# Sandwich transformer kernel, rotation tables made on GpSimd for two blocks at once, and the second residual placed inside the root step on VectorE

## What is computed

```python
x = attn_layer(shift_tokens(x), Wqkv[i], q_scale[i], k_scale[i], Wo[i]) + x   # first residual
x = ffn_layer(shift_tokens(x), ...) + x                                      # second residual

q = l2norm(q) * qs ;  k = l2norm(k) * ksc
q = q * cos * scale + rotate_half(q) * sin * scale
k = k * cos * inv   + rotate_half(k) * sin * inv
out = local_attention(q, k, v)      # windows of 32 tokens, 16 heads of 64
```

## Time and profile before

| | us |
|---|---|
| median of 3 runs | 1886.04 (1882.17 to 1889.05) |
| the profiled execution: its time | 1887.05 |
| the profiled execution: its span | 1885.2 |

### The profile page before, as it was taken

How to read it: one execution, slowest core, us unless ns; L and a number is a source line. 1 busy time by engine, 2 the same in 40 slices (tenths; PEclk the granted TensorE clock), 3 DMA queues, 4 the chain that set the end, 5 groups by cost and what they waited for, 6 DMA issues and landing times. The chain is left out here.

```text
span 1885.2 us, 76475 instructions
## 1 busy us (share of the span) xinstructions
PE 1674.5 (89%) x30960; PEld 1193.9 (63%) x30960; DVE 1578.2 (84%) x2345; ACT 1221.7 (65%) x2072; POOL 1483.0 (79%) x819
## 2 busy tenths in 40 slices
PE   3946878899999999999999999999999999999974
PEld 2523556666766676667667666676676766776663
DVE  5787767789889898898998888989989889898854
ACT  3334556567677776777777767777767677776753
POOL 1638767778888888888888888888888888888841
PEclk8878989999999999999999999999999999999997
DMA  3001131122223222323221332222242223222210
GB/s 133 1 1 45 49 99 48 47 67 60 63 74 104 58 56 64 78 69 89 64 67 45 87 102 67 67 53 70 67 111 57 54 67 78 66 58 65 67 47 23
DMA packets 80698, 121.88 MB, mean 65 GB/s; under 512 B 16776, under 2 KB 29574, under 8 KB 79750
## 3 DMA queue, kind: packets, MB, share of 16 engines
q1 hardware_dynamic: 80646, 121.14, 24.4%
HBM read 19.36 MB, written 1.05 MB: 11 GB/s over the span
## 5 line engine op out<-in xcount | busy, mean ns | idle before, releaser
L729 PE MATMUL r<-wqkv,xs 128*128 (+1 forms) x1152 | 561.2, 618 | 13.0 <-DVE rot_sin L1246 3.7
L1433 POOL TENSOR_TENSOR rot<-rot,root 128x1024 f32<-128x1024 f32 x192 | 377.9, 1988 | 120.6 <-DVE root L1284 120.6
L1405 POOL TENSOR_TENSOR rot<-rot,rot_sin 128x1024 f32<-128x1024 f32 x192 | 451.8, 2365 | 1.2 <-DVE rot_sin L1246 1.2
L729 PEld LDWEIGHTS r<-wqkv,xs 128*128 128x128 f32 x1152 | 210.5, 196 | 213.0 <-issue 197.6
L1079 ACT ACTIVATE squares<-r 128x512 f32<-128x512 f32 x384 | 217.6, 598 | 83.9 <-PE r L729 82.8
L1235 DVE TENSOR_TENSOR rot<-r,table 128x1024 f32<-128x1024 f32 x192 | 232.7, 1212 | 23.0 <-PE r L734 10.2
L1418 POOL TENSOR_TENSOR squares<-squares 128x512 f32<-128x512 f32 x192 | 244.8, 1275 | 9.0 <-ACT squares L1079 8.8
L1449 POOL TENSOR_TENSOR probs<-probs,rinv 128x1024 f32<-128x1024 f32 x96 | 182.8, 1905 | 81.0 <-DVE rinv L1306 81.0
L1246 DVE TENSOR_TENSOR rot_sin<-r,table 128x512 f32<-128x512 f32 x384 | 242.6, 672 | 0.0
L734 PE MATMUL r<-square,rot 128*128 128x128 f32 x1536 | 208.1, 279 | 19.5 <-POOL rot L1433 14.0
L734 PEld LDWEIGHTS r<-square,rot 128*128 128x128 f32 x1536 | 169.5, 141 | 83.8 <-issue 29.9
(11 more groups left out here) (125 smaller groups left out, 2688.5 us busy)
## 6 DMA issues: line engine op xcount, KB each, us to landing
vwin<-vtok SPq DMA_DIRECT2D x576, 128.0 KB, 2.3
vwin<-vtok SPq DMA_DIRECT2D x384, 64.0 KB, 2.0
wqkv<-in_wqkv SPq DMA_DIRECT2D x6, 1536.0 KB, 8.3
wo<-in_wo SPq DMA_DIRECT2D x6, 512.0 KB, 4.9
w<-in_w SPq DMA_DIRECT2D x6, 341.0 KB, 3.0
x<-in_x SPq DMA_DIRECT2D x4, 256.0 KB, 3.7
rope<-in_rope SPq DMA_DIRECT2D x1, 1024.0 KB
out_x<-y SPq DMA_DIRECT2D x4, 256.0 KB, 2.3
```

What stands on the lines that cost most here:

```text
L729: pe.matmul(dst[:, c * 512:(c + 1) * 512], xs1[:, u, :], w.rearrange("p a n -> p (a n)"), start=True, stop=True).then_inc(S[done], 1)
L1405: pool.tensor_tensor(r, r, rot_sin[:, k, :, :, :].rearrange("p h a d -> p h (a d)"), ALU.add)\
L1433: pool.tensor_tensor(r, r, bcast(root[:, at:at + HEADS], 2, DH), ALU.mult)\
```

## The change

Two things are changed. The table product leaves DVE: POOL makes it, for both blocks of a pair in one instruction of 128x512, one pair ahead, between `fold_q` 1 and `weigh` 0; the table has a second buffer that pairs take in turn, so the DVE readers pick theirs by an address computed at run time. And `find_roots` is split: `residual2` now stands behind the first root step and ahead of the seed.

```diff
-        table = sb("table", [P, 2, 4, DH])
+        table = sb("table", [P, 2, 2, 4, DH])
...
             def turn_cos(n, u, k, src, squared, turned, transposed):
-                dve.wait_ge(S["tabled"], n + 1)
+                dve.wait_ge(S["tabled"], n // 2 + 1)
...
-                                  bcast(table[:, u, 2 * k, :], 1, HEADS), ALU.mult).then_inc(S[turned], 1)
+                                  bcast(table[:, bass.ds((n // 2) % 2, 1), u, 2 * k, :].rearrange("p a d -> p (a d)"),
+                                        1, HEADS), ALU.mult).then_inc(S[turned], 1)
...
-                    sin = table[:, u, 2 * k + 1, 32 * a:32 * a + 32]
+                    sin = table[:, bass.ds((n // 2) % 2, 1), u, 2 * k + 1, 32 * a:32 * a + 32]\
+                        .rearrange("p a d -> p (a d)")
...
-                    tables(2 * m, 0)
-                    tables(2 * m + 1, 1)
...
-                    find_roots(m)
+                    begin_roots(m)
                 if runs(m - 4):
                     residual2(m - 4)
+                if runs(m) or runs(m - 2):
+                    finish_roots(m)
...
+            def tables(m):
+
+                if not isinstance(m, int) or m >= 2:
+                    pool.wait_ge(S["q_turned"], 6 * (m - 1))
+                    pool.wait_ge(S["k_turned"], 6 * (m - 1))
+                pool.tensor_tensor(table[:, bass.ds(m % 2, 1), :, :, :].rearrange("p a u k d -> p (a u) (k d)"),
+                                   rope[:, bass.ds((m % PPB) * 2, 2), :, :].rearrange("p a k d -> p a (k d)"),
+                                   bcast(scales[:, bass.ds(m // PPL, 1), :, :].rearrange("p a k d -> p (a k d)"), 1, 2),
+                                   ALU.mult).then_inc(S["tabled"], 1)
...
                     fold_q(2 * m + 1, 1)
+                if runs(m + 1):
+                    tables(m + 1)
...
-            run(pool, step)
+            pool.wait_ge(S["tables_loaded"], 7 * 16)
+            tables(0)
+            run(pool, step, PAIRS - 1)
```

More of the change, by code:

```diff
@@ L653, in first, with run @@
             return isinstance(n, int) and n == 0
-        def run(eng, step):
+        def run(eng, step, end=PAIRS):
             for m in range(FILLED):
                 step(m)
-            with eng.Fori(FILLED, PAIRS) as m:
+            with eng.Fori(FILLED, end) as m:
                 step(m)
-            for m in range(PAIRS, PAIRS + BEHIND):
+            for m in range(end, PAIRS + BEHIND):
                 step(m)
@@ L1253, in norm_square, with begin_roots @@
                                   [:, :, 0, :], AX.X, ALU.add).then_inc(S[summed], 1)
-            def find_roots(m):
+            def begin_roots(m):
                 before = ROOT_OPS * m
@@ L1267, in find_roots, with finish_roots @@
                        .then_inc(S["refined"], 1 if runs(m) else 2)
+            def finish_roots(m):
+                before = ROOT_OPS * m
                 dve.wait_ge(S["refined"], before + 2)
```

## The result

| | us |
|---|---|
| changed kernel, median of 4 runs | 1913.35 (1909.4 to 1916.38) |
| kernel before beside it, median of 4 runs | 1887.55 (1882.17 to 1892.4) |
| ratio | 1.0136, 95% interval 1.0101 to 1.0171 |
| profiled execution of the changed kernel: time, span | 1914.91, 1913.1 |

What follows compares the result with a forecast made beforehand. The bound was taken to be a loop through several engines, none full. 42 x 0.56 = 23.5 less 41 x 0.26 = 10.7 gives +12.8 us, with +0.3 for start and end: median 1899, 8-in-10 range 1879 to 1910.

Steps and rivals of the forecast that it cites:

- Gain on `turn_q` 1: On PE, `turn_q` 1 no longer waits for DVE's tables to free r0: 0.26 us gained a step.
- POOL's product: Table product on POOL ahead of `weigh` 0: 1.27 us, covered by idle before `weigh` 1, cost on the loop 0.
- the estimate weighed beside it: From the skill's GpSimd page: POOL's product takes 1.6 us, PE loses 0.3 a step, total 13 us higher.
- The register work of the table's readers: Twelve table readers with run-time addresses, 0.10 to 0.26 us each, hidden where the engine is busy: taken as 0.
- both gains: 0.26 us on `turn_q` 1 and some 0.3 on POOL's scales: POOL free for the product at about 933.9.
- `residual2` in the roots: On DVE the seed waits behind residual2, which waits for `ff_down`: 0.56 us a step, wholly on the loop.
- The step that failed: PE's idle 1.25 us before `ff_up` 0 is not on the loop, since `turn_q` 0 waits for the scale anyway.
- The drain: In steps behind the loop residual2 no longer follows nine Newton instructions: worth under 1 us, +0.3 together with the start.
- The first cos product: On DVE, expected directly behind the roots, with DVE's idle time up by about 3.5 us a step.
- A, the residual hides: Residual2 fits before the seed's wait for POOL ends: cost 0, gain 0.26 stays, -11 us, 1875; 15 in 100.
- B, a wash: Residual2 costs 0.18 against 0.26, 1883; or `turn_q` 1 gains 0.5 against 0.56, 1889; 22 in 100.
- C, POOL's product as the brake: Product at 2.34 us delays `weigh` 1 and PE, `ff_down` some 0.8 later: 34 us on top, 1933; 7 in 100.

Runs made afterwards that it cites:

- the pair with `ff_up` 0 issued twice: Matmuls of `ff_up` 0 issued twice in the changed kernel, 1898.92 us, and in the kernel before with only residual2 moved, 1910.22 us.
- the one with less work: Kernel with only the tables moved, half of `ff_up` 0 left out and one q 0 projection matmul cut from 512 to 128 columns: 1891.59 us.
- the fast kernel: Changed kernel with residual2 put back behind the roots, so only the tables are on POOL: 1872.88 us.
- the run with fixed addresses: Changed kernel with residual2 at fixed addresses, writing over its own PSUM input, so x is not updated: 1884.35 us.
- the run behind `weigh` 0: Kernel with only the tables moved, POOL's table product placed behind `weigh` 0 instead of ahead of it: 1873.47 us.
- the run behind `weigh` 1: Kernel with only the tables moved, POOL's table product placed behind `weigh` 1 instead of ahead of `weigh` 0: 1935.0 us.

## Why the prediction was right in its steps and wrong in its sum

**The loop and its terms.** These held. Gain on `turn_q` 1: 0.26 forecast, 1.13 to 0.87 measured, 0.32 a step in all with the tables alone. POOL's product: 1.27 forecast, 1.28 measured and not the 1.6 of the estimate weighed beside it, with 0.51 idle left before `weigh` 1 (0.5 forecast). The register work of the table's readers, put at 0, shows no cost: with it the step still gained the 0.32. Two figures beside the sum were off: with both gains counted POOL would have been free for the product at 933.6 and not 933.9, and DVE's busy time fell by 30.49 - 25.15 = 5.3 us a step and not by some 3.5, since the seed no longer waits for POOL. The timeline of POOL in the changed kernel:

```profile
975.96 1.28 POOL L1416 TENSOR_TENSOR squares<-squares 128x512 f32<-128x512 f32 x1
977.19 1.28 POOL L1450 TENSOR_TENSOR table<-rope,scales  x1
978.42 1.91 POOL L1457 TENSOR_TENSOR probs<-probs,rinv 128x1024 f32<-128x1024 f32 x1
980.85 1.91 POOL L1457 TENSOR_TENSOR probs<-probs,rinv 128x1024 f32<-128x1024 f32 x1 [0.51 <-DVE rinv L1304]
```

`residual2` in the roots: 0.56 forecast, 3.09 - 2.50 = 0.59 measured, and the distance from `ff_down` 0.43 forecast, 988.69 - (986.66 + 1.56) = 0.47 measured. In the timelines of PE and DVE:

```profile
986.66 1.56 PE L827 MATMUL pm<-hid,w 128*128 128x256 f32 x6 [0.18 <-DVE minus_half L1261]
...
988.69 0.48 DVE L1332 SCALAR_TENSOR_TENSOR xT<-pm,cols,mid 128x256 f32 x1 [2.25 <-PE pm L827]
989.09 0.19 DVE L1272 TENSOR_SCALAR root<-minus_half 128x67 int32<-128x67 int32 x1
...
995.00 1.23 DVE L1228 TENSOR_TENSOR rot<-r,table 128x1024 f32<-128x1024 f32 x1 [3.35 <-PE r L734]
```

The step came out at 34.41 for 34.44.

**The step that failed** is the sentence on PE's idle time: "That idle is not on the loop: `turn_q` 0 behind it waits for the scale anyway." As a wait it is not. The idle before `turn_q` 0 was even foreseen, but priced at nothing, and the sum held every PE duration at what it was in a kernel whose loop has the clock at 1.00. With 2.45 us not busy in a step instead of 1.73, TensorE's clock fell eight times in the loop, which is 14.1 us that stand nowhere in the sum, and was lower in the drain. The runs that tell this from a wait are the pair with `ff_up` 0 issued twice: the same steps, no long ones, and loops 14.0 and 17.7 us shorter; and the one with less work, which has the step of the fast kernel and the drops of the slow one. Why idle time lowers the clock in just these steps is not shown.

**The drain** was put at under 1 us, and with the start at +0.3; it cost 4.85. Ahead of the `turn_q` 0 behind the last scale of the loop PE had idled 3.47 us, and it ran at the lower clock:

```profile
1826.70 1.94 PE L734 MATMUL r<-square,rot 128*128 128x128 f32 x8 [3.47 <-POOL rot L1431]
```

```profile
1824.66:1913.10 88.44, 54.83 (x828) 43.10 (x828) 35.23 (x75) 36.95 (x59) 20.10 (x12) 0.79 0.11 30
```

The eight transposes take 1.94 us there, 1.10 in the loop. The same stretch of the kernel before has a clock of 0.87, and PE busy 50.56 of its 83.59 us. With `ff_up` 0 issued twice the stretch takes 85.80 us at a clock of 0.85, so at least 2.6 of the 4.85 go with the idle time and the clock; that the clock makes up the rest is argued, not shown by a run. The fill, 1.9 us shorter, hid a part of this; by the scatter of the fill between executions that is luck.

**The first cos product** was to start directly behind the roots with the tables gone. It does not: it waits 3.35 us for `turn_q` 0, which must have read `rot` before the product may overwrite it. In the kernel before, `turn_q` 0 ended at 915.88 + 1.09 = 916.97 and the tables at 914.81 + 3.34 = 918.15, so only some 1.2 us of their 3.58 were not covered by this wait, and taking them away frees little, whatever their 150 us of busy time. The forecast's sum did not use that sentence, since it had taken 0.26 from `turn_q` 1 alone.

**The rivals.** A, the residual hides, needed an earlier first root step: the run with fixed addresses shows the residual at a cost of 0.16 even at the shortest distance, close to the 0.18 given as the lower bound. B, a wash, would have been that case, 1884 (forecast 1883). C, POOL's product as the brake, fell with the product's 1.28 (close to the 1.3 from which it was to decide) and with the run behind `weigh` 0, which changed nothing; the run behind `weigh` 1 gives its mechanism a price. No case had a loss beyond the sum of the waits, and that is why the range ended at 1910.

**Better than both kernels** is the change without the residual's move: 1872.88 us, 0.67% under the kernel before.

## What to carry to other kernels

Busy time taken off an engine is worth only what the next reader of its result waited for. Here 150 us of DVE's time were worth 13. An instruction put into a chain of small dependent ones costs its wait too, and an address found at run time behind that wait comes on top. And where TensorE is nearly full, its idle time has a price though nothing waits for it: read the granted clock of single steps, count the time in which PE is not busy before and after a change, and look whether PE's work at the place of a drop is on the loop.

## What the runs showed of the hardware

- With PE at its higher clock and 2.0 us of idle before one group in every step, the granted clock fell to the lower level in some steps and not in others, at nearly even distances; each such step was 1.2 to 1.8 us longer in four kernels, while in a fifth all but one of seven drops fell ahead of idle time of PE and cost nothing (35.03 us against 35.02). Filling the idle time with matmuls issued a second time made the changed kernel's loop 14.0 us faster (medians 1913.35 and 1898.92); taking matmuls away made one loop 14.4 us slower (medians 1872.88 and 1891.59).
- An address computed at run time, placed behind a semaphore wait on DVE, adds 0.43 us between the end of the matmul waited for and the instruction (0.47 against 0.04).
- DVE and POOL hold each other up without a semaphore. The seed takes 2.20 us where POOL's `add_k` runs, 0.19 where it starts behind it; the first root step 1.05 or 2.39, by which of POOL's two adds it meets; the two tables 3.34 or 3.82. POOL's three scales take 5.99 beside the tables, 5.62 without them. The Trainium skill, SBUF — State Buffer, section "Who interferes with whom", says that DVE in its two-port modes, or with two inputs in SBUF while GpSimd reads SBUF, shares a pair of ports with GpSimd, and that the second to issue is blocked until the first is done. The trace agrees in its ends: the seed ends at 911.49 and POOL's `add_k` at 911.43, the first root step at 909.18 and `add_q` at 909.09; the second table ends 0.3 us behind POOL's second scale.
